# Reordering the head of a two-layer GNN kernel: layer-norm rows, key weights in two column halves, head norms and key scores

## The reference, cut to what matters

```python
h = relu(layernorm(x))                       # x is 1250 x 512
x = x + L0(h)                                # layer 0
x = x + L1(relu(layernorm(x)))               # layer 1: aggregate over edges, two matmuls, batch norms

def L0(h):
    xn = batchnorm(h)
    agg = mean of xn[src] over the edges that end in each node      # 20,000 edges
    conv_out = relu(agg @ W_conv + b_conv)
    q, k, v = h @ Wq, h @ Wk, h @ Wv         # 256 kept positions, 8 heads of 64
    u = phi's scores: (t * scale) @ proj.T   # 256 random features for q and for k
    qf = exp(u_q - |q|^2/2 - rowmax) / 16 + keps
    kf = exp(u_k - |k|^2/2 - max over the whole head) / 16 + keps
    attn = (qf @ (kf.T @ v)) / (qf @ sum(kf))
    return batchnorm(conv_out + attn @ Wo + h)
```

## Time and the profile before

| | us |
|---|---|
| median of three runs (345.0 to 345.96) | 345.02 |
| the profiled execution | 345.06 |
| its span in the profile | 343.2 |
| TensorE busy | 330.9 (96%) |
| VectorE busy | 217.0 (63%) |
| ScalarE busy | 165.9 (48%) |
| GpSimd busy | 117.1 (34%) |

### The profile page before, as it was taken

One profiled execution on the slowest core, in us unless ns is written; L12 is line 12 of the kernel. 1 busy time (PEld: TensorE's weight loads), 2 busy tenths in 40 slices (PEclk: granted clock), 3 DMA queues, 4 the chain that ended last, 5 costly groups with the idle time before them and its releaser, 6 DMA issues.

```text
span 343.2 us, 5827 instructions
## 1 busy us (share of the span) xinstructions
PE 330.9 (96%) x2130; PEld 212.5 (62%) x2130; DVE 217.0 (63%) x479; ACT 165.9 (48%) x265; POOL 117.1 (34%) x200
## 2 busy tenths in 40 slices
PE   8999899999999999999988989999999999999994
PEld 4788556777676576775656754555555555566562
DVE  4879998878968548779878866123555344332325
ACT  2458766362471594724577674114445462513032
POOL 4333179552200010000517887221665644101100
PEclk9999999999999999999999999999999999999999
DMA  6993306000000000648000000000000000020223
GB/s 198 275 248 133 125 10 235 4 2 3 0 3 2 2 3 1 221 132 196 0 2 1 2 0 4 2 0 0 3 0 3 0 1 2 0 62 15 75 62 90
DMA packets 13480, 18.15 MB, mean 53 GB/s; under 512 B 1542, under 2 KB 6848, under 8 KB 13444
## 3 DMA queue, kind: packets, MB, share of 16 engines
q1 hardware_dynamic: 13095, 17.40, 17.9%
q10 hardware_dynamic: 349, 0.26, 0.2%
HBM read 15.10 MB, written 2.56 MB: 51 GB/s over the span
## 4 chain that ended last, share of the span: by engine, by line
PE 81%; DVE 8%; POOL 4%; ACT 2%; issue 2%; DMA 1%; DVEq 0%; SPq 0%; POOLq 0%; ACTq 0%
PE bank L1412 76%; PE bank L1448 2%; POOL hn L554 1%; PE bank L1801 1%; POOL ln_s L514 1%; DMA edge<-dst 1%; PE bank L1760 1%; DVE st_row L1300 1%; ACT hh L844 1%; PE bank L1618 1%; DVE x L1363 1%; DVE st L1103 0%; DVE aggf L1320 0%; DVE ring L997 0%; DVE hl L1281 0%
## 5 line engine op out<-in xcount | busy, mean ns | idle before, releaser
L1412 PE MATMUL bank<-AT,hh 125*128 125x400 f16 (+3 forms) x250 | 81.1, 332 | 1.0 <-DVE hl L1281 0.6
L1412 PE MATMUL bank<-AT,hl 125*128 125x400 f16 (+3 forms) x250 | 80.8, 331 | 0.0
L1412 PEld LDWEIGHTS bank<-AT,hh 125*128 125x128 f16 x250 | 24.1, 97 | 19.3 <-issue 1.1
L1412 PEld LDWEIGHTS bank<-AT,hl 125*128 125x128 f16 x250 | 24.2, 97 | 17.8 <-issue 0.2
L1412 PE MATMUL bank<-a_hi,w_hi 128*128 128x400 f16 (+1 forms) x96 | 32.6, 339 | 0.0
L1412 PE MATMUL bank<-agg_hi,w_hi 128*128 128x400 f16 (+1 forms) x96 | 32.6, 339 | 0.0
L1412 PE MATMUL bank<-a_hi,w_lo 128*128 128x400 f16 (+1 forms) x96 | 32.5, 338 | 0.0
L1412 PE MATMUL bank<-agg_hi,w_lo 128*128 128x400 f16 (+1 forms) x96 | 32.5, 338 | 0.0
L1412 PE MATMUL bank<-agg_lo,w_hi 128*128 128x400 f16 (+1 forms) x96 | 32.5, 338 | 0.0
L1412 PE MATMUL bank<-a_lo,w_hi 128*128 128x400 f16 (+1 forms) x96 | 32.5, 338 | 0.0
L604 POOL TENSOR_TENSOR a_lo<-zr,a_hi 128x1250 f16<-128x1250 f32 x7 | 22.0, 3140 | 16.7 <-DVE a_hi L1334 16.7
(11 more groups left out here) (222 smaller groups left out, 720.9 us busy)
## 6 DMA issues: line engine op xcount, KB each, us to landing
w_s<-w SPq DMA_DIRECT2D x4, 1024.0 KB, 5.1
x<-x SPq DMA_DIRECT2D x2, 1120.0 KB
x_in<-x SPq DMA_DIRECT2D x4, 448.0 KB
out<-x SPq DMA_DIRECT2D x6, 224.0 KB
wB<-wk SPq DMA_DIRECT2D x1, 1024.0 KB, 9.4
wA<-wq SPq DMA_DIRECT2D x1, 1024.0 KB, 13.3
wC<-w_conv SPq DMA_DIRECT2D x1, 1024.0 KB, 13.7
wB<-wv SPq DMA_DIRECT2D x1, 1024.0 KB, 8.8
```

What stands on the lines that cost most here:

```text
L1412: return pe.matmul(o, l, r, start=start, stop=stop, skip_group_check=True)
```

## The change

It touches the head of the kernel, up to about 60 us.

```diff
-    "hT0 hT1 hT2 K0", "K1", "hT3 hT4 PT Q0", "hT5 hT6 N1 Q1 hT7", "hT8 N0 hT9 UK0", "P", "FR UQ0 V0", "MX0 V1", "QT0",
-    "G0 UK1", "KV0 UQ1 G1", "O0 G2", "G3 MX1", ...
+    "hT0 hT1 hT2 K0", "K1", "hT3 hT4 PT Q0", "hT5 hT6 N1 Q1 hT7", "N0 UK0 hT8 hT9", "P", "FR UQ0 V0", "MX0 V1", "QT0",
+    "UK1 G0", "KV0 UQ1 G1", "O0 G2", "G3 MX1", ...
-SPARE = {"start": 18, "chosen": 7, "hT0": 3, "hT1": 2, "hT2": 3}
+SPARE = {"start": 18, "chosen": 5, "hT0": 3, "hT1": 1, "hT2": 3}
@@ SyncE
-            sp.dma_start(wB[:], w_t(wk)).then_inc(sem("d_wB"), 16)
+            for half in range(2):
+                cols = slice(half * D // 2, (half + 1) * D // 2)
+                sp.dma_start(wB[:, :, cols], w_t(wk)[:, :, cols]).then_inc(sem(f"d_wk{half}"), 16)
...
-            sp.dma_start(wB[:], w_t(wv)).then_inc(sem("d_wB"), 16)
+            sp.dma_start(wB[:], w_t(wv)).then_inc(sem("d_wv"), 16)
@@ ScalarE
             rows(0)
             rows(1)
+            rows(2)
             rows_T(0)
-            rows(2)
             rows_T(1)
@@ TensorE
-                    pe.wait_ge(sem("d_wB"), 32)
+                    pe.wait_ge(sem("d_wv"), 16)
...
-                    w, d, n = (wA, "d_wA", 16) if name[0] == "Q" else (wB, "d_wB", 16)
-                    pe.wait_ge(sem(d), n)
+                    w, d = (wA, "d_wA") if name[0] == "Q" else (wB, f"d_wk{name[1]}")
+                    pe.wait_ge(sem(d), 16)
```

## The result

The changed kernel takes 346.1 us (median of 12 executions, 345.51 to 349.73), the kernel before 345.4 in its 12 beside it. The ratio is 1.0041, 95% interval [1.0021, 1.0060]: 0.4% slower, as 346.4 from 345.02 (1.0040) had it. That agreement is in part luck. The medians lie only 0.7 us apart; the averages, 346.7 and 345.45, lie 1.25 us apart because three long executions are in the first. The order's price was smaller than I had worked out, a cost that I had left out made up for it, and the small term for the packets had the wrong sign.

A forecast was written before the change was run, and what follows sets the result against it. TensorE's queue and its standstills bound the kernel (81% of the span). Rows, fillers and half 0 at 0, packets +0.1, UK1 ahead of G0 +1.25 sum to +1.35: 345.02 to 346.4 us, range 345.2 to 347.3.

The forecast's parts named there:

- The order's price: Slot 9, UK1 ahead of G0: window 9's count 1.25 us later, slot 4's 0.46 us gain already included.
- the small term for the packets: W_k's transfer as 1,024 packets of 1 KB for 512 of 2 KB: tile 3 lands 0.1 us later, at most 0.57.
- `UK1` ahead of `G0` waits for the exponentials: Slot 9: UK1 needs banks 2 and 3, held until ScalarE's exponentials end; TensorE idle some 1.9 us, UK1 at 53.45.
- The rival by which `UK1` fits into the standstill: Slot 9: UK1 fills TensorE's wait for hn, 1.5 us gained, 343.6 us; needs the banks free by 50.6; chance 0.08.
- Slot 4: Window 4's count 1.4 us earlier, 1.2 of it returned as a wait at FR; VectorE gains 0.46 us.
- Rows and fillers at 0: Kernel head: third row earlier and three fillers fewer cost 0; K0 moves between 0.3 us earlier and 0.25 later.
- the cover that I named, the flag: Window 0's count waits for VectorE's flag, hiding K0's shift; without it the edits are worth at most 0.16 us.
- my list of TensorE's standstills: Four idle notes: window 0's count 0.16 us, hT8 1.47, G0 0.43, KV1 0.33.
- Lower bound: 0, since bytes are equal: W_k's smaller packets: the least delay of tile 3 is 0, as the bytes stay the same.
- The clock: Rival: TensorE's clock falls to 1.2 GHz through UK1 and G0, 4.7 us taking up to twice as long, up to 351; chance 0.03.

The follow-up runs named there:

- e1_g0_first: The changed kernel with slot 9 put back to G0 UK1, all else kept: ratio 0.9995 to the kernel before, median 345.39 us.
- e9_fr_filler: The changed kernel with slot 9 put back to G0 UK1 and 5 filler matmuls ahead of FR: ratio 0.9976 to the kernel before, median 344.8 us.
- e8_both_fillers: The changed kernel with 5 filler matmuls ahead of FR and 8 ahead of UK1: ratio 1.0025 to the kernel before.
- e2b_uk1_filler: The kernel before with slot 9 as UK1 G0 and 8 filler matmuls in the pause ahead of UK1: ratio 1.0062 to the kernel before.
- e7_split_later_uk1: The changed kernel with VectorE's low half of W_conv one window later, so nbk comes earlier: ratio 1.0021 to the kernel before.
- e5_rows_fill_only: The kernel before with only ScalarE's third row ahead of the first copy and the two filler counts lowered: ratio 0.9999.
- e3_slot4_only: The kernel before with only slot 4 reordered to N0 UK0 hT8 hT9: ratio 1.0003.
- e4_halves_only: The kernel before with only W_k transferred in two column halves: ratio 0.9996.
- e10_fr_filler_split: All of the change but slot 9, 5 fillers ahead of FR, low half of W_conv one window later: ratio 0.9977 to the kernel before, median 344.32 us.
- e11_uq0_split: All of the change but slot 9, UQ0 ahead of FR, low half of W_conv one window later, 4 fillers ahead of G0: ratio 0.9991 to the kernel before.

## Why the prediction was right, step by step

- **`UK1` ahead of `G0` waits for the exponentials.** Right, place, releaser and nearly the size: a pause of 1.71 us for 1.9, `UK1` at 53.13 for 53.45, window 9 at 57.73 for 58.14. `e1_g0_first` removes the loss with this one edit (and `e9_fr_filler` does, beside `e8_both_fillers`), `e2b_uk1_filler` brings it by itself at 1.66 us for 1.7, and `e7_split_later_uk1` moves it by moving what it waits for. The rival by which `UK1` fits into the standstill is out: the banks are free at 52.94, not at 50.6. The price by itself was 1.66 us, as worked out; what was mis-sized is what VectorE takes off it (next point).
- **Slot 4.** Right: the 1.4 us that TensorE wins at window 4 end in a wait at `FR`, and VectorE's gain reaches `G0`. The pause at `FR` was 0.78 us instead of 1.2; `FR` itself came 0.38 us earlier instead of 0.15, of which 0.10 was there at window 1 already. The size of VectorE's gain was wrong: I took its wait in one execution, 0.46 us, for what it can gain. Where the x tiles come in time that wait is 0.61 (`e5_rows_fill_only`), the reduction starts 0.69 earlier since window 1 in the changed kernel, and windows 1 to 9 win 0.71 (`e9_fr_filler`). In `e3_slot4_only` the late tiles took 0.31 of it: its reduction starts 39.47 - 23.52 = 15.95 us after window 1, for 37.84 - 22.20 = 15.64 in the changed kernel. So the net price was 0.84 us in the profile and some 0.9 by `e8_both_fillers`, where my term had 1.25.
- **Rows and fillers at 0.** Right as far as the times can tell (`e5_rows_fill_only`). `K0` came 0.52 us later, but the order's own part is 0.15, within my range. In the changed kernel the cover that I named, the flag, was gone, and `K0` itself held window 0's count. The cover had also been thicker than the 0.16 us of the idle note: where `K0` holds the count it follows 3.53 us behind `K0`'s start (18.23 - 14.70), and before it was 3.85 (18.03 - 14.18), so the flag held it by 0.32. In my list of TensorE's standstills `K0`'s own wait of 0.26 us was missing, and the one at 76.22 lies outside the first 60 us.
- **The packets, +0.1 us.** The step that failed is "Lower bound: 0, since bytes are equal". I reckoned with the mean price of a packet, but what is waited for is the end of the whole transfer. That end came earlier with halves, by 0.9 us on average, and tile 3 with it: VectorE never waited for it. The sign was wrong. The Trainium skill's rule ("DMA: Bandwidth & Descriptors", "Why small descriptors are slow (HBM only)"), by which W_k would take longer in 1 KB packets, isn't what these transfers show either: the end came at 12.8 for 13.9 us in the two kernels' profiles. By themselves the halves show no gain in time (0.9996, `e4_halves_only`).
- **The clock.** I gave it 0.03, because a pause of 1.47 us had left it at 1.00. That one row was no proof. The kernel before was below 0.995 in 4 of 90 executions beside the experiments, the changed one in 3 of 12, the same with `nbk` earlier in 2 of 12, with slot 9 put back in 5 of 12, slot 4 alone in 4 of 12, slot 9 alone in 6 of 6. With fillers in the pauses it was so in none of 12, 12, 8 and 6 executions. This was a second cost with a share of the executions, not a rare rival. It didn't come as I had it, up to 4.7 us at once, but at 1.6 us where a profile shows it. The nine executions at a high clock average 0.6 us above the kernel before (346.06 for 345.45), and the three long ones bring that to 1.25: so the smaller order price and this cost together gave the forecast 0.4%. That is luck.

What stays open: why column halves shorten the end of the transfer, and how much each of the two pauses adds to the three long executions of the changed kernel. Those lie 1.8 to 3.7 us above the average of the other nine, more than one fall of 1.6 us in two of the three, and none of them was profiled. Nor is every long execution the clock's: one of `e4_halves_only` (347.35 us) and one of `e5_rows_fill_only` (347.22) had a clock of 0.996.

## What to carry to other kernels

Before a group is moved ahead of a pause, look up when its output buffer comes free, not only when its inputs are ready. A dependency that is never waited for today, because a later place covers it, has no row in the profile; here it was found by comparing the end of `UK0`'s exponentials with the start of `G0`. And a pause on TensorE has a second price: if it can't be closed, filler matmuls on a bank that is free anyway keep the granted clock, and only with them did the good half of this change show. They are free only as far as the pause is long: five ahead of `FR` left it where it was (17.76 us after window 1 for 17.74), four ahead of `G0`, where no pause was left, cost 0.77 us.

## What the hardware showed that I had not expected

- A pause of 0.78 us on TensorE ahead of `FR` was followed by a granted clock of 0.63 from 42 to 46 in one execution of `e1_g0_first` and by 1.00 in the profiled one of the changed kernel. The same pause is paid or not from one execution to the next. A fall cost about 1.6 us each time that a profile shows one: `V0` 5.27 for 3.70, `UK1` and `G0` together 6.43 for 4.84.
- One 1 MB transfer cut into two column halves landed on average 0.9 us earlier at its end (13.0 us in eight profiles for 13.9 in five), with twice the packets. From one execution to the next the end of the same transfer moved by up to 1.9 us (13.0 to 14.9).
- GpSimd's four `hn` operations took 4.91 or 4.92 us where VectorE's operation on W_conv (2.45 us, L1240) ran beside them, and 2.88 or 2.89 us in the three runs that moved it one window later (`e7_split_later_uk1`, `e10_fr_filler_split`, `e11_uq0_split`). The four `hn` operations of the next tile, beside which it then ran, took 5.99 to 6.01 us, for 3.95 in the changed kernel. The prediction had counted on nothing changing there.
